# Expert values added to their token rows by accumulating scatters, with the attention's score blocks reordered by a table

## The reference

```python
def _softmax_attention(xn):                 # B=4, S=2048, D=256, 16 heads of width 16, no mask in effect below
    Q, K, V = xn @ Wq + bq, xn @ Wk + bk, xn @ Wv + bv; Q, K = rope(Q), rope(K)
    score = einsum("bsid,bsjd->bsij", Q, K) / sqrt(16)   # heads against heads, within one token
    return einsum("bsij,bsjd->bsid", softmax(score), V)
def _ffn(xn):
    x = xn + mla(rmsnorm(xn, g1))           # latent attention, causal over S, 16 heads
    t = rmsnorm(x, g2)
    logits = t @ gate_w                     # 8 experts
    gates = softmax(top_2(logits))
    ye = silu(t @ w1[e]) @ w2[e]            # 256 -> 512 -> 256
    return x + sum over the two chosen e of gate_e * ye_e
xn = layernorm(x)
out = x + _softmax_attention(xn) + _ffn(xn)
```

## Time and profile before

| | |
|---|---|
| median of 3 runs | 3087.91 us (3085.34 to 3088.96) |
| profiled execution | 3105.57 us, span 3104.0 us, clock 0.925 |
| PE busy | 2541.4 us (82%) |
| DVE busy | 2341.3 us (75%) |
| POOL busy | 2252.2 us (73%) |
| ACT busy | 1544.4 us (50%) |
| DMA | 435.67 MB, 140 GB/s mean |

### The profile page before, as it was taken

How to read it: one execution, slowest core, us unless ns; L and a number is a source line. 1 busy time by engine, 2 the same in 40 slices (tenths; PEclk the granted TensorE clock), 3 DMA queues, 4 the chain that set the end, 5 groups by cost and what they waited for, 6 DMA issues and landing times. The chain is left out here.

```text
span 3104.0 us, 60116 instructions
## 1 busy us (share of the span) xinstructions
PE 2541.4 (82%) x21392; PEld 1305.4 (42%) x21392; DVE 2341.3 (75%) x3764; ACT 1544.4 (50%) x2314; POOL 2252.2 (73%) x1218
## 2 busy tenths in 40 slices
PE   7998968999999999999999999757759888889400
PEld 4544433333333333333333332146647777777400
DVE  4567759888898888988889885035549999999243
ACT  2322236767776767776777777612224444444100
POOL 5443349898989899999989899837736666666476
PEclk9999989999999999999999999967679999999755
DMA  6886542323233232322233211167567666666675
GB/s 191 275 260 210 168 143 56 84 52 83 81 87 76 61 84 78 87 69 70 82 85 86 57 57 42 37 218 244 187 216 213 205 205 204 206 208 211 214 235 187
DMA packets 346973, 435.67 MB, mean 140 GB/s; under 512 B 40858, under 2 KB 276860, under 8 KB 346748
## 3 DMA queue, kind: packets, MB, share of 16 engines
q1 hardware_dynamic: 300796, 350.81, 38.3%
q0 software_dynamic: 17920, 54.55, 5.3%
q10 hardware_dynamic: 28032, 27.27, 2.5%
HBM read 273.43 MB, written 158.47 MB: 139 GB/s over the span
## 5 line engine op out<-in xcount | busy, mean ns | idle before, releaser
L1013 DVE TENSOR_REDUCE p_piece_max<-p_ring 128x1 f32<-128x512 f32 (+3 forms) x2160 | 1281.7, 653 | 186.5 <-PE p_ring L158 97.5
L1071 ACT ACTIVATE p_probs<-p_st 128x1024 f32<-128x1024 f32 (+3 forms) x1280 | 1076.7, 894 | 451.5 <-PE p_st L1134 238.7
L1134 PE MATMUL p_st<-unit_q,unit_k 64*128 64x512 bf16 (+3 forms) x3520 | 417.4, 348 | 27.0 <-SPq L865 17.3
L1152 PE MATMUL p_pv<-p_probs,unit_vg 128*32 128x512 f32 (+3 forms) x3520 | 412.1, 545 | 0.0
L1759 POOL TENSOR_TENSOR p_pv<-p_pr,p_qkv 128x4096 f32<-128x4096 f32 x32 | 347.8, 10868 | 36.3 <-ACT p_pr L1857 35.6
L942 POOL TENSOR_TENSOR p_terms<-p_head_p,p_head_in 128x4096 f32<-128x4096 f32 x32 | 347.8, 10868 | 0.3
L158 PE MATMUL p_ring<-unit_k,unit_q 64*128 64x512 bf16 (+3 forms) x1600 | 272.9, 354 | 69.0 <-DVE p_piece_max L1013 68.6
L1930 PE MATMUL p_y_ps<-p_w,p_hid 128*128 128x256 f32 x1152 | 276.4, 395 | 30.0 <-ACT p_hid L1870 30.0
L921 POOL TENSOR_TENSOR p_terms<-p_head_in 128x4096 f32<-128x4096 f32 x32 | 283.0, 8844 | 7.0 <-POOL p_head_s L929 4.4
L948 POOL TENSOR_TENSOR p_terms<-p_terms 128x2048 f32<-128x2048 f32 (+2 forms) x96 | 252.6, 2631 | 17.1 <-POOL p_terms L948 11.4
L926 POOL TENSOR_TENSOR p_terms<-p_terms 128x2048 f32<-128x2048 f32 (+2 forms) x96 | 252.2, 2627 | 17.2 <-POOL p_terms L926 11.5
(11 more groups left out here) (188 smaller groups left out, 3678.8 us busy)
## 6 DMA issues: line engine op xcount, KB each, us to landing
p_w<-ffn_w SPq DMA_DIRECT2D x144, 512.0 KB, 5.3
qk_parts<-p_parts SPq DMA_DIRECT2D x64, 384.0 KB, 3.5
head_qkv<-p_heads SPq DMA_DIRECT2D x16, 1536.0 KB, 6.4
p_rows<-sorted_rows SPq DMA_DIRECT2D x72, 256.0 KB, 4.1
expert_rows<-p_y ACTq DMA_DIRECT2D x72, 256.0 KB, 5.6
unit_q<-qk_parts SPq DMA_DIRECT2D x132, 128.0 KB, 3.2
unit_k<-qk_parts SPq DMA_DIRECT2D x132, 128.0 KB, 3.7
p_x<-attn_x SPq DMA_DIRECT2D x32, 512.0 KB, 5.4
```

The lines of the kernel that those rows point to most:

```text
L1013: nc.vector.tensor_reduce(piece_max[:, n % 2, h:h + heads, i, pc], ring_ps[g % RING][:, 0:heads * width].rearrange("p (h k) -> p h k", h=h ...
L1071: nc.scalar.activation(probs[:, 2 * turn_of(s, i) + u, :, 0:width], st_ps[u][:, :, 0:width], ACT.Exp).then_inc(probs_done, 1)
L1134: last = nc.tensor.matmul(st_ps[u][:, half, 0:width], k6[s][rows, PAIR * second + u, kt * P:(kt + 1) * P], q6[s][rows, PAIR * second + u, ...
L1152: last = nc.tensor.matmul(pv_ps[hh * VW:(hh + 1) * VW, skip:CT], vg[s][:, kt, hh * VW:(hh + 1) * VW], probs[:, 2 * turn_of(s, i) + hh % PA ...
```

## The change

- The combining stage goes. A DRAM tensor `acc` holds the sum: routing writes residual plus the head attention of the attention stage's 32 blocks; in the experts' stage POOL adds each tile's rows to their tokens' rows by two accumulating indirect scatters (`add_tile`) and each head block by an accumulating store (`add_block`). Both wait until the adds before them have landed, since the adds read and write the same rows. ACT multiplies by the gate as it copies from PSUM. The last stage copies `acc` to `out` in 16 transfers on SP and ACT.
- Gate and token number travel as two more columns of each scattered row (258 instead of 256), twice per token, with a copy by ACT (`copy_th`). Row and value buffers go from two to four; 71 tiles instead of 72; the table stays in SBUF.
- In the experts' stage the scores of a head block are in PSUM, DVE finishes an older block first, and POOL's weighting is cut into a half and two quarters, with the adds between.
- Attention: the pairs stand by a written table, three places a step (behind each of the two score blocks and behind the values). Head blocks are loaded and stored by SP.
- Borders: rows of ones earlier, one value store a chunk instead of four, the first chunk of routing loaded at the end of attention, and POOL's first two RMS inverses ahead of the multiply that waits for the last unit's sums.

```diff
-                for g in range(NG):
-                    sp.dma_start(v_dram[b, g, ...], vx[:, s, :, g * HG:(g + 1) * HG, :]...).then_inc(vx_stored[s], 16)
+                sp.dma_start(v_rows[b, c * CT:(c + 1) * CT, :]..., vx[:, s, :, :, :]...).then_inc(vx_stored[s], 16)
...
-    ISSUED = [[issued(n, i) for i in range(N_STEP)] for n in range(UNITS)]
+    OTHER_UNITS = """
+        100 100 010 101 011 010 011 011 011 111 011 010 011 010 010 111 011 011 011 011
...
                     scores(n, s, i, 0)
+                    maxima(done, ends[0])
                     scores(n, s, i, 1)
-                    maxima(done, cut)
+                    maxima(ends[0], ends[1])
                     if i >= LAG:
                         values(n, s, i - LAG)
-                    maxima(cut, upto)
+                    maxima(ends[1], ends[2])
...
+            sp.dma_start(wo[:, :, :], w["ffn_Wo"]...).then_inc(wo_loaded, 16)
+            sp.dma_start(first_oT[:, :, :], o_v[0, 0]).then_inc(first_loaded, 16)
+            sp.dma_start(first_xn[:, :, :], xn_v[0, 0]).then_inc(first_loaded, 16)
+            sp.dma_start(first_x[:, :, :], x_v[0, 0]).then_inc(first_loaded, 16)
             store_o(UNITS - 1, NC - 1)
             store_values(UNITS - 2)
-            for slot in range(2):
-                wait_apart(sp, o_stored[slot], ...)
-            wait_apart(sp, quotient_steps, QUOTIENT_STORED * (UNITS - 1), apart)
...
+            inverse_rms(0)
+            inverse_rms(1)
             wait_apart(pool, last_quotient, RAW_LANDED, apart)
             nc.gpsimd.tensor_tensor(raw[:, :], raw[:, :], spread[:, :], ALU.mult).then_inc(last_quotient, 1)
-            inverse_rms(0)
-            inverse_rms(1)
...
+                nc.scalar.copy(th[:, c, 1, :, 0:D], th[:, c, 0, :, 0:D]).then_inc(th_copied, 1)
...
+            def add_tile(n, i, blocks):
+                wait_apart(pool, y_copied, n + 1, apart)
+                if not (static(n) and n == 0):
+                    wait_apart(pool, y_added, 16 * RT * n, apart)
+                if not (static(blocks) and blocks == 0):
+                    wait_apart(pool, oh_added, 16 * blocks, apart)
+                for t in range(RT):
+                    nc.gpsimd.indirect_dma_start(
+                        acc, bass.IndirectOffsetOnAxis(rows[:, i, t, D + 1:].bitcast(U32), 0), y[:, i, t, :], None,
+                        compute_op=ALU.add).then_inc(y_added, 16)
+
+            def add_block(m, u, n, tiles):
+                wait_apart(pool, oh_done, m + 1, apart)
+                wait_apart(pool, y_added, 16 * RT * tiles, apart)
+                nc.gpsimd.dma_start(acc[bass.ds(n * P, P), :], oh[:, u, :, :]...,
+                                    accum_op=ALU.add).then_inc(oh_added, 16)
+            def body(g):
+                for i in range(tiles_of(g)):
+                    n = 4 * g + i
...
+                        add_tile(n - 1, (i - 1) % RB, ...)
+                    if weigh and i % 2 == 0:
+                        weigh_values(m, u, slice(0, H // 2), False)
+                    if weigh and i % 2:
+                        weigh_values(m, u, slice(H // 2, 3 * H // 4), False)
+                    done = 2 * g + i // 2 - 2
+                    if i % 2 and (not static(g) or 0 <= done < NB):
+                        add_block(done, i // 2, 4 * g - 4 + 2 + i // 2, n)
+                    if weigh and i % 2:
+                        weigh_values(m, u, slice(3 * H // 4, H), True)
...
-                nc.vector.tensor_reduce(s[:, :, :], prod[:, :, :, :], AX_X, ALU.add).then_inc(s_done, 1)
+                nc.vector.tensor_reduce(s_ps[u], prod[:, :, :, :], AX_X, ALU.add).then_inc(s_done, 1)
...
-                    act.wait_ge(y_stored[u], 16 * (2 * g + i // 2))
+                    if not static(g) or g:
+                        act.wait_ge(y_added, 16 * RT * (n - RB + 1))
                     for t in range(RT):
-                        last_copy = nc.scalar.copy(y[:, u, t, :], y_ps[t][:, 0:D])
+                        last_copy = nc.scalar.activation(y[:, i, t, :], y_ps[t][:, 0:D], ACT.Copy, scale=rows[:, i, t, D:D + 1])
...
 def phase5_combine(nc, apart, res_v, attn_v, pos_v, gates_v, expert_rows, out_v):
+    acc = SHARED["acc"][0:T, :].rearrange("(b c t p) d -> b c t p d", b=B, c=NC, p=P)
+        def store(eng, i):
+            for b in range(B):
+                for c in range(i * NC // 2, (i + 1) * NC // 2):
+                    eng.dma_start(out_v[b, c].rearrange("p t d -> t p d"), acc[b, c]).then_inc(stored[i], 16)
+            wait_apart(eng, stored[i], 16 * B * NC // 2, apart)
```

More of the change, by code:

```diff
@@ L60, with block_of @@
 UNITS = HEAD_BLOCKS // 2
+RW = D + 2
+def block_of(m, half):
+    return 4 * (m // 2) + 2 * half + m % 2
 def wait_apart(eng, sem, value, apart):
@@ L865, in _ @@
             sp.sem_inc(neg_stored, 64)
+            for u in range(2):
+                load_heads(u, u)
             set_ones(sp, k6[2], ones, ones_set)
@@ L995, in _ @@
             divide(UNITS - 2)
-            for u in range(2):
-                wait_apart(pool, head_stored[u], 16 * UNITS, apart)
         @block.vector
@@ L1270, in phase3_route @@
         th_done = sem("p3_th_done")
+        th_copied = sem("p3_th_copied")
+        attn_loaded = [sem(f"p3_attn_loaded{c}") for c in range(NC)]
+        attn_added = sem("p3_attn_added")
         tT_done = sem("p3_tT_done")
@@ L1451, in _ @@
                 scale_rms(0, c, c)
+            dve.wait_ge(last_inverse, SUMS_LANDED)
+            nc.vector.reciprocal(inverse[:, :], sums[:, :]).then_inc(last_inverse, 1)
             def body(b, c, n, ahead):
@@ L1575, in body @@
                     squares(n + 2)
+                if ahead >= 1:
+                    copy_th(*after(b, c + 1), n + 1)
             chunks(act, body)
@@ L1688, in phase4_experts @@
         y_copied = sem("p4_y_copied")
-        y_stored = [sem(f"p4_y_stored{i}") for i in range(2)]
+        y_added = sem("p4_y_added")
         qkv_loaded = [sem(f"p4_qkv_loaded{i}") for i in range(2)]
@@ L1701, in phase4_experts, with static, tiles_of, has_blocks @@
         oh_done = sem("p4_oh_done")
-        oh_stored = [sem(f"p4_oh_stored{i}") for i in range(2)]
+        oh_added = sem("p4_oh_added")
         block = ctx.enter_context(nc.Block())
         def quads(eng, body):
-            body(0, True, True, False)
-            with eng.Fori(1, QUADS) as g:
-                body(g, True, False, False)
+            body(0)
+            body(1)
+            with eng.Fori(2, QUADS) as g:
+                body(g)
             for g in range(QUADS, ALL_QUADS):
-                body(g, False, g == QUADS, g == ALL_QUADS - 1)
+                body(g)
+        def static(g):
+            return isinstance(g, int)
+        def tiles_of(g):
+            return IN_LAST if static(g) and g == ALL_QUADS - 1 else 4
+        def has_blocks(g):
+            return not static(g) or g < QUADS
         @block.sync
         def _(sp):
-            sp.dma_start(table_sb[:, :, :], table.unsqueeze(0)).then_inc(w_loaded, 16)
-            def load_block(m, u):
+            def load_block(m, u, n):
                 wait_apart(sp, prod_done, m + 1, apart)
@@ L1771, in _ @@
[L1771 to L1780 removed]
+                h = rows_of_heads
+                count = h.stop - h.start
+                ins = nc.gpsimd.tensor_tensor(
+                    pv[:, u, h, :, :],
+                    pr[:, u, h, :].unsqueeze(2).to_broadcast([P, count, DH, H]),
+                    qkv[:, u, 2, :].rearrange("p (j d) -> p d j", d=DH).unsqueeze(1).to_broadcast([P, count, DH, H]),
+                    ALU.mult)
@@ L1857, in probabilities, with body @@
                 nc.scalar.activation(pr[:, u, :, :], sm[:, :, :], ACT.Exp).then_inc(exp_done, 1)
+            copy_rows(0)
             copy_q(0, 0, 1)
             copy_q(1, 1, 1)
-            copy_rows(0)
-            def body(g, has_blocks, first, last):
-                for i in range(4):
-                    n, u = 4 * g + i, i % 2
+            def body(g):
+                for i in range(tiles_of(g)):
+                    n = 4 * g + i
                     for k in range(2):
@@ L1932, in second, with body @@
                 last.then_inc(y_done, 1)
-            transpose_rows(0, 0, 0)
-            def body(g, has_blocks, first, last):
-                for i in range(4):
+            transpose_rows(0, 0, 1)
+            def body(g):
+                for i in range(tiles_of(g)):
                     n, u = 4 * g + i, i % 2
                     hidden(n, u, 2 * g + i // 2)
-                    if not (last and i == 3):
-                        transpose_rows(n + 1, 1 - u, 2 * g + (i + 1) // 2)
+                    if not (static(n) and n == N_TILE - 1):
+                        transpose_rows(n + 1, (i + 1) % RB, g + 1 + (i + 1) // RB)
                     second(n, u)
@@ L1971, in _ @@
+    with SHARED["stack"], ExitStack() as ctx:
+        stored = [ctx.enter_context(nc.semaphore(f"p5_stored{i}")) for i in range(2)]
```

(11 more changed lines are left out.)

462 lines of the change are left out of this document (211 added, 251 removed).

## The result

The changed kernel took 3061.88 us in the median of 7 runs (3056.19 to 3075.31), against 3088.61 us of the kernel before in 7 runs: ratio 0.992, 95% interval 0.9907 to 0.9933. It is faster by 27 us (0.8%, clear of the noise but small), where 158 were forecast, and 3061.88 lies outside the range of 2855 to 3015.

What follows compares the result with a forecast made beforehand. Each stage has its own limit: PE in attention, POOL in routing and combining, DVE's chain in the experts' stage. Terms -8 - 42 - 32 + 76 - 152 = -158 gave 2948 us profiled, 2930 as median; range 2855 to 3015.

Steps and rivals of the forecast that it cites:

- Experts' stage: Experts' stage: POOL sets the turn at 19.7 us, 32 turns, 702 us against about 626, so +76.
- four scatters at 0.96 + 0.30 ... That is 17.1 us with nothing waited for: POOL's work a turn in the experts' stage: weighting 10.9, four scatters 5.6, block's add 0.6 us.
- Landings: Experts' stage: POOL's adds wait for earlier ones to land, 3.7 us for a scatter, 4.3 for the block's add.
- The scatter in the middle: Experts' stage: this scatter has half the weighting, 5.4 us, as cover and waits for nothing.
- landings hidden: Rival, experts' stage: both adds land within 2.7 us, turn 17.1, stage 619, total time 2847 us; chance 0.2.
- late landings: Rival, experts' stage: adds land so late the kernel is slower, from a turn of 24.6 us; chance 0.1.
- The difference: DVE's difference in the experts' stage: with scores in PSUM it falls from 3.2 to 0.4 us.
- the 16 chunks stay at POOL's 12.5 us: Routing, between first and last scatter: POOL keeps its pace of 12.5 us a chunk, no change.
- Start of routing: Border from attention to routing: multiply at 2043, first scatter at 2047, so -28 us (bounds -15 and -35).
- Attention: Table of pairs in the attention: half the ring waits return, 3 us a unit for 14 units, -42 us.
- the waits only move: Attention, lower bound for the table of pairs: the ring waits only move and nothing is gained.
- Last stage: Combining's 192 us go; copying 8.4 MB at 240 GB/s takes 35 us plus 5, so -152 (bounds -164 and -111).

Runs made afterwards that it cites:

- the first experiment: The kernel before with one edit, the scores of a head block in the experts' stage in PSUM instead of SBUF: 3027.5 us, ratio 0.9801.

## Why the prediction was wrong

Right in its direction and in its picture (POOL takes over the turn from DVE, with waits for landings), wrong in its largest term. The miss of the sum is 114.5 us: 82 in the experts' stage, 19 between the scatters, 12.5 in the attention, 9.5 ahead of the first scatter, 2 in smaller steps, less 10.6 that the last stage gained more. The median adds 17.

- **Experts' stage, "four scatters at 0.96 + 0.30 ... That is 17.1 us with nothing waited for": this is the step that failed.** POOL's own work in a turn was forecast at 17.1 us and is 19.44, and 31 turns times 2.34 are 73 of the 82 us. The price of an adding scatter was taken from a plain one, and bounds were drawn only for the landing. With plain writes the work is 16.87, near the forecast's 17.1. So cutting the weighting costs next to nothing; of the 2.57 us of adding the four scatters make 2.36 and the block's store 0.2. The waits were forecast at 2.6 us a turn and are 2.6, but that sum came in part by luck, as the next point says.
- **Landings: the sum right, its parts not.** The scatter was taken to land 3.7 us behind its end. Its median of 5.1 from issue, 3.5 behind its end, is near that. But the one that counts, just ahead of the block's add, landed about 6.9 from issue in the 24 turns that waited, so about 5.4 behind its end. The block's add was taken at 4.3 us behind an end of 0.6, 4.9 from issue, and landed at 3.1. So POOL waited 59.2 / 31 = 1.9 us a turn ahead of the block's add where 1.0 were forecast, and at most 12.7 / 31 = 0.4 behind it where 1.6 were: two errors of opposite sign. The scatter in the middle, forecast to wait for nothing, waited too in some turns (as at 2411.42, 0.89 us). Of the rival "landings hidden" the block's half came and the scatter's did not; the turn of 22.04 rules it out. Rival "late landings" did not come: its turn of 24.6 was not reached.
- **DVE.** The difference is at 0.42 us and the product stands still behind a half, as forecast (4.75 us at 2363.70, beside the half from 2362.11). The run with scores in SBUF shows that DVE has at least 1.25 us a turn to spare, so the difference does not decide.
- **Routing, "the 16 chunks stay at POOL's 12.5 us": failed.** DVE waited 24.6 us for stores of rows, which have two buffers, 9.6 of them gone with the blanks out of the way, and stood 20 us at the jumps of its loop, which the prediction did not look at. That POOL sets a stage's pace before does not say how much slack the engines behind it have.
- **Start of routing.** Forecast -28, measured -18.5. The path from SP's gather to the multiply was taken at 24 us and took 25.3 (1990.02 to 2015.32), the scatter 4 us behind it is right too. The failed part is "it starts about then again": the gather left 12.5 us behind PE's last values before (2006.4 to 2018.90) and 20.8 now, since SP issues the loads of three chunks ahead of it, one of which took 4.17 us to issue. A move within one queue has a price for what stands behind it.
- **Attention.** -42 forecast as half of the ring waits; -29.5 measured, of which 22.6 by the table and 7 by edits that were not made alone. The ring waits fell from 100.6 to 35.2 us, and the waits for ACT rose from 8.6 to 32.1: "the waits only move" held for a third.
- **Last stage.** 28.6 us instead of 40: 8.4 MB in 28.59 us at 293 GB/s in the profile's row, where 240 were taken and 5 us around it.
- **Profile and median.** The 17.7 us were taken off at the end, as if the changed kernel's profiled execution would lie as far above its median. It lies 0.4 above: two thirds of the 17.7 us stood ahead of the experts' stage, in rows against which gains were counted. In the trace of before DVE has nine waits of 38 us in all in its routing loop that the first experiment's trace lacks; what they wait for the trace does not tell.

## What to carry to other kernels

When the change has a new form of an instruction, here the same scatter with an addition, that form needs its own bounds for the time on the engine that issues it, beside those for its landing; multiply both by the number of turns before believing a gain from a stage that goes. Before an edit is judged by a change that holds it, make it alone: the scores in PSUM gained 62 us where DVE was the limit and nothing where POOL was. When a store must wait for another's landing, ask first whether the two need the same tensor; a place of its own was worth 64 us here, and keeping the blocks in SBUF about 35 more (47 less the 12 of the loop). Read a turn as a mean over its whole loop: one turn of 17.95 us stood for a mean of 17.31, and 31 of them made 20 us.

## What the runs showed of the hardware

- An adding indirect scatter of 128 rows of 1 KB kept POOL 0.6 us longer than a plain one (records of 1.58 against 0.96 to 1.02 us), landed 1.8 us later (5.1 against 3.3 us from issue), and POOL's transfers had three times the packets (145 against 48). The packets alone do not explain the longer instruction. With the store adding and the scatters plain there are 7056 packets for 21 stores and 84 scatters (2450 to 2850), which is 144 and 48 each; the adding store has them too, and cost POOL 0.2 us (17.08 against 16.87). It landed at 3.1 us from issue in the changed kernel, the plain one at 2.9 in the run with all writes plain. What makes the scatter longer stays open.
- DVE's difference, with both operands in SBUF, took 3.2 us on average beside POOL's weighting, and 0.42 us with one of them in PSUM. In the changed kernel it took 1.67 us in SBUF and 0.42 in PSUM.
- DVE's jump back in a long loop came with two stops of 5 us at each of two jumps in all nine traces with the new routing loop; in the two with it written out there were none. In the trace of before, whose loop has the same three turns, the longest stop in issue is 1.7 us. Why the jump is dear only in the new loop stays open.
- A copy of 8.4 MB from DRAM to DRAM in 16 transfers on two queues took 28.6 us with all that is around it, 293 GB/s by the bytes copied.
